# Attention and hidden layer on eight cores: the last two token tiles one by one, bias rows by an accumulating DMA, query weights loaded sooner

## The reference, cut to what matters

```
x = x + attn(layernorm(x))
    q = r @ query_proj (16 heads);  k = r @ key_proj;  v = r @ value_proj
    out = softmax(q k^T / 8) v, then @ output_proj
x = x + ffn(layernorm(x))
    s = r @ Win + bin                      # 64 features
    h = relu(s[..., None] * W1 + b1)       # 64 x 16
    g = sum(h * W2, over the 16) + b2
    out = g @ Wout + bout                  # 1,024 features
```

## Time and profile before

| what | us |
|---|---|
| three runs shown | 969.11, 969.49, 1022.97 (median 969.49) |
| the profiled execution | 971.45 |
| its spans, cores 0 to 7 | 968.6, 967.3, 969.1, 965.8, 969.9, 965.9, 966.7, 966.5 |
| slowest core | core 4, mean granted TensorE clock 0.981 |
| busy on core 4 | PE 900.7, ACT 913.9, DVE 646.1, POOL 72.2 |

### The profile page before, as it was taken

How to read it: one execution, slowest core, us unless ns; L and a number is a source line. 1 busy time by engine, 2 the same in 40 slices (tenths; PEclk the granted TensorE clock), 3 DMA queues, 4 the chain that set the end, 5 groups by cost and what they waited for, 6 DMA issues and landing times.

```text
span 969.9 us, 29153 instructions; the slowest of 8 cores (965.8 to 969.9 us)
## 1 busy us (share of the span) xinstructions
PE 900.7 (93%) x11484; PEld 479.2 (49%) x11484; DVE 646.1 (67%) x938; ACT 913.9 (94%) x1000; POOL 72.2 (7%) x150
## 2 busy tenths in 40 slices
PE   3899999999999999998999999998999998998895
PEld 3445555554445554554555554554454454454442
DVE  4756777522469999988889899658332378748225
ACT  2599999999999999999999999999999999999971
POOL 3211112100000000000010000000000000100000
PEclk9999999999999999999999999999999999999995
DMA  8722346400100010001031000001130100500101
GB/s 194 183 73 89 110 142 135 97 2 2 28 18 19 18 19 17 3 7 51 29 115 18 18 18 14 7 7 50 36 108 18 29 13 7 180 18 18 50 2 44
DMA packets 46291, 48.71 MB, mean 50 GB/s; under 512 B 35152, under 2 KB 35280, under 8 KB 46160
## 3 DMA queue, kind: packets, MB, share of 16 engines
q1 hardware_dynamic: 38352, 27.71, 10.4%
q0 software_dynamic: 7520, 18.62, 7.6%
q10 hardware_dynamic: 288, 0.52, 0.1%
HBM read 35.70 MB, written 8.39 MB: 45 GB/s over the span
## 4 chain that ended last, share of the span: by engine, by line
ACT 78%; issue 11%; PE 7%; DVE 2%; DMA 2%; POOL 0%; DVEq 0%; SPq 0%; ACTq 0%; POOLq 0%
ACT ptu L1163 77%; PE ob L731 2%; DMA xbuf<-x_own 1%; PE spa L1030 1%; DMA wqb<-wq 1%; PE spb L1030 1%; PE spb L1067 0%; PE spa L1067 0%; PE sdb L664 0%; DVE lnst L753 0%; DVE lnst L757 0%; PE sdb L695 0%; PE sda L695 0%; ACT hz L1173 0%; DVE gacc L1132 0%
## 5 line engine op out<-in xcount | busy, mean ns | idle before, releaser
L1163 ACT ACTIVATE ptu<-spa 128x1024 bf16<-128x1024 f32 x491 | 555.3, 1131 | 11.5 <-PE spa L1030 11.3
L1163 ACT ACTIVATE ptu<-spb 128x1024 bf16<-128x1024 f32 x490 | 555.8, 1134 | 3.6 <-PE spb L1030 3.3
L731 PE MATMUL ob<-vab,ptu 128*128 128x65 bf16 x7848 | 391.7, 195 | 3.4 <-DVE oacc L943 1.1
L731 PEld LDWEIGHTS ob<-vab,ptu 128*128 128x128 bf16 x7848 | 286.7, 98 | 203.8 <-issue 203.8
L1030 PE MATMUL spb<-qt,k2t 64*128 64x512 bf16 x980 | 193.5, 382 | 19.4 <-ACT ptu L1163 18.0
L1030 PE MATMUL spa<-qt,k2t 64*128 64x512 bf16 x982 | 193.6, 383 | 17.9 <-ACT ptu L1163 14.9
L1030 PEld LDWEIGHTS spb<-qt,k2t 64*128 64x128 bf16 x980 | 58.7, 92 | 110.7 <-issue 95.9
L1030 PEld LDWEIGHTS spa<-qt,k2t 64*128 64x128 bf16 x982 | 57.7, 93 | 108.5 <-issue 95.0
L943 DVE TENSOR_TENSOR oacc<-oacc,ob 128x520 f32<-128x520 f32 x52 | 35.8, 689 | 76.4 <-PE ob L731 76.3
L1184 POOL TENSOR_SCALAR lnve<-lnmv 128x1 f32<-128x1 f32 x48 | 14.9, 311 | 582.1 <-DVE lnmv L759 582.0
L929 DVE SCALAR_TENSOR_TENSOR r1t<-oacc 128x1024 bf16<-128x1024 f32 x43 | 52.6, 1223 | 5.2 <-DVE oacc L924 4.7
(11 more groups left out here) (136 smaller groups left out, 705.3 us busy)
## 6 DMA issues: line engine op xcount, KB each, us to landing
xbuf<-x_own SPq DMA_DIRECT2D x16, 512.0 KB, 5.2
xbuf<-x_oth SPq DMA_DIRECT2D x16, 512.0 KB, 3.4
out<-xbuf POOLq DMA_DIRECT2D x14, 512.0 KB, 3.1
xbuf<-x_own POOLq DMA_DIRECT2D x12, 512.0 KB, 7.1
wqb<-wq POOLq DMA_DIRECT2D x8, 256.0 KB, 9.3
xtra<-x_own SPq DMA_DIRECT2D x4, 512.0 KB, 6.6
xtra<-wp POOLq DMA_DIRECT2D x8, 256.0 KB, 4.7
ot<-on SPq DMA_TRANSPOSE x38, 2.3
```

The lines of the kernel that those rows point to most:

```text
L731: r = te.matmul(osum[:, hd, c * 65:(c + 1) * 65], ptu[:, g % NPT, hd * 512 + c * 128:hd * 512 + (c + 1) * 128], vab[:, CHUNKS[s][i], :], s ...
L1163: sc.activation(ptu[:, g % NPT, :], sps[g % 2][:], AF.Exp, scale=0.125 / SCORE_SCALE).then_inc(ex, 1)
```

## The change

Five things are changed.

1. GpSimd issues the value weights and query chunk 1 after the root of the second tile, chunk 2 after the third and chunk 3 after the fourth. VectorE normalizes the second tile ahead of the third tile's statistics. `AT_FIRST` is 1.4 us less.
2. The second pass of the final additions is gone. GpSimd issues, once a tile is normalized, a DMA that adds boutbc to the tile in xbuf (both in on-chip memory), and the first final addition of a tile waits for it. The new semaphores stand for four buffers.
3. In the tail the one-row bias matmuls are gone, and tiles 14 and 15 get their bias by the same DMA.
4. In the tail VectorE adds and takes statistics for both tiles, then normalizes both. The hidden layer is computed for one tile after the other, with 128 columns.
5. The four sums of tile 14 stand ahead of VectorE's move of tile 15's transposes, the other twelve behind it.

```diff
-AT_FIRST = {"pe": 2100, "dve": 2200}
+AT_FIRST = {"pe": 1960, "dve": 2060}
...
                     xh = xbuf[:, t, b * 512:(b + 1) * 512]
+                    if b == 0:
+                        v.wait_ge(bad[t], 16 * (a // 4 + 1))
                     v.tensor_tensor(xh, xh, bank[:], op=ALU.add).then_inc(sev, 1)
-                    note("sev", n + 1)
-                    yield [], 75
-                    v.wait_ge(sev, n + 1)
-                    if a == 0 and b == 0:
-                        v.wait_ge(boutl, 16)
-                    v.tensor_tensor(xh, xh, boutbc[:, b * 512:(b + 1) * 512], op=ALU.add).then_inc(bad, 1)
...
-            for n, t in enumerate(GROUPS[-1]):
-                te.wait_ge(xad, n + 1)
-                for h in range(2):
-                    te.matmul(sps[t % 2][:, h * 512:(h + 1) * 512], ones1[:],
-                              boutbc[0:1, h * 512:(h + 1) * 512], start=True, stop=False)
...
+            def hidden(n, t):
+                te.wait_ge([rta, rtv][n], 1)
+                for j in range(DCH):
+                    r = te.matmul(obk[:, 512 * n:512 * n + 128], winb[:, j, :],
+                                  r2t[:, j, t % 4 * 128:t % 4 * 128 + 128],
+                                  start=(j == 0), stop=(j == DCH - 1))
+                r.then_inc(s2t, 1)
...
+            ta, tb = GROUPS[-1]
+            transposes(0, ta)
+            hidden(0, ta)
+            transposes(1, tb)
+            hidden(1, tb)
+            ffn_out(0, ta)
+            ffn_out(1, tb)
...
             ln_stats(v, 1)
             ln_norm(v, 0)
+            ln_norm(v, 1)
             ln_stats(v, 2)
-            ln_norm(v, 1)
             ln_stats(v, 3)
...
                 v.wait_ge(xad, n + 1)
                 ln_stats(v, li)
-                ln_norm(v, li)
+            for t in GROUPS[-1]:
+                ln_norm(v, NTILES + t)
...
+            for p in range(4):
+                hidden_sum(0, p)
             v.wait_ge(rtt, 2)
             v.tensor_copy(r2t[:, :, 384:512], side[1][:, :].bitcast(BF16).rearrange("p (j t) -> p j t", t=128)
                           ).then_inc(rtv, 1)
+            for p in range(4, 8):
+                hidden_sum(0, p)
             for p in range(8):
...
+                hidden_sum(1, p)
+            for n, t in enumerate(GROUPS[-1]):
+                v.wait_ge(bad[t % 4], 16 * NK)
...
+        def add_bout(e, t):
+
+            if t == 0:
+                e.wait_ge(boutl, 16)
+            e.wait_ge(nrm, NTILES + t + 1)
+            e.dma_start(xbuf[:, t % 4, :], boutbc[:], accum_op=ALU.add).then_inc(bad[t % 4], 16)
...
-                if i == 2:
+                if i == 1:
                     e.dma_start(wvb[:], wv_d.rearrange("p (j m) -> p j m", m=64)).then_inc(wvl, 16)
-                for c in {2: [1], 3: [2, 3], 4: [4], 5: [5], 6: [6], 7: [7]}.get(i, []):
+                for c in {1: [1], 2: [2], 3: [3], 4: [4], 5: [5], 6: [6], 7: [7]}.get(i, []):
...
                 for t in ts:
-                    e.wait_ge(bad, 2 * t + 2)
+                    add_bout(e, t)
+                for t in ts:
+                    wait_ev(e, USE_NO["fo", t, 1])
                     e.dma_start(out_r[t], xbuf[:, t % 4, :]).then_inc(ost[t % 4], 16)
```

More of the change, by code:

```diff
@@ L533, in build_nc @@
         rsd = sem("rstd_set")
-        bad = sem("bout_added")
+        bad = [sem(f"bout_added{q}") for q in range(4)]
         b1s = sem("b1adj_set")
@@ L1063, in _, with transposes @@
                 r.then_inc(opt, 1)
-            for n, t in enumerate(GROUPS[-1]):
-                te.wait_ge(xad, n + 1)
-                for h in range(2):
-                    te.matmul(sps[t % 2][:, h * 512:(h + 1) * 512], ones1[:],
-                              boutbc[0:1, h * 512:(h + 1) * 512], start=True, stop=False)
+            def transposes(n, t):
                 te.wait_ge(nrm, NTILES + t + 1)
@@ L1074, in _, with ffn_out @@
                 r.then_inc(rtt, 1)
[L1075 to L1082, removed]
+            def hidden(n, t):
[5 more added lines that the diff above has]
+                r.then_inc(s2t, 1)
+            def ffn_out(n, t):
+                te.wait_ge(g2c, len(GROUPS) + n)
                 for h in range(2):
@@ L1085, in _ @@
                               g2b[:, t % 4 * 128:(t % 4 + 1) * 128], woutb[:, h * 512:(h + 1) * 512],
-                              start=False, stop=True).then_inc(fot, 1)
+                              start=True, stop=True).then_inc(fot, 1)
+            ta, tb = GROUPS[-1]
[5 more added lines that the diff above has]
+            ffn_out(1, tb)
         @block.vector
@@ L1119, in _, with hidden_sum @@
                 ln_stats(v, li)
-                ln_norm(v, li)
+            for t in GROUPS[-1]:
+                ln_norm(v, NTILES + t)
+            def hidden_sum(n, p):
+                cols = slice(128 * n, 128 * n + 128)
+                last = slice(256 + 128 * n, 384 + 128 * n)
+                v.wait_ge(rel, 8 * n + p + 1)
+                dst = g2b[:, last] if p == 7 else gacc[p % 2][:, cols]
+                if p == 0:
+                    v.tensor_scalar(dst, zt[p % 4][:, cols], w2p[:, p:p + 1], b2h[:], op0=ALU.mult,
+                                    op1=ALU.add).then_inc(gtl, 1)
+                else:
+                    v.wait_ge(gtl, 7 * n + p)
+                    v.scalar_tensor_tensor(dst, zt[p % 4][:, cols], w2p[:, p:p + 1],
+                                           gacc[(p + 1) % 2][:, cols],
+                                           op0=ALU.mult, op1=ALU.add).then_inc(g2c if p == 7 else gtl, 1)
+            for p in range(4):
+                hidden_sum(0, p)
             v.wait_ge(rtt, 2)
@@ L1123, in _ @@
                           ).then_inc(rtv, 1)
+            for p in range(4, 8):
+                hidden_sum(0, p)
             for p in range(8):
[L1125 to L1134 removed]
+                hidden_sum(1, p)
+            for n, t in enumerate(GROUPS[-1]):
+                v.wait_ge(bad[t % 4], 16 * NK)
                 for h in range(2):
[L1136 removed]
+                    v.wait_ge(fot, 2 * n + h + 1)
                     xh = xbuf[:, t % 4, h * 512:(h + 1) * 512]
@@ L1168, in _ @@
                           AF.Copy).then_inc(rta, 1)
-            sc.wait_ge(s2t, 1)
-            for p in range(8):
-                if p >= 4:
-                    sc.wait_ge(gtl, p - 3)
-                sc.activation(zt[p % 4], obk[:, 0:256], AF.Relu, bias=b1adj[:, p:p + 1],
-                              scale=w1p[:, p:p + 1]).then_inc(rel, 1)
+            for n in range(2):
+                sc.wait_ge(s2t, n + 1)
+                for p in range(8):
+                    if p >= 4:
+                        sc.wait_ge(gtl, 7 * n + p - 3)
+                    sc.activation(zt[p % 4][:, 128 * n:128 * n + 128], obk[:, 512 * n:512 * n + 128], AF.Relu,
+                                  bias=b1adj[:, p:p + 1], scale=w1p[:, p:p + 1]).then_inc(rel, 1)
             for n, t in enumerate(GROUPS[-1]):
@@ L1221, in _ @@
                 rstd_of(e, NTILES + t)
+            for t in GROUPS[-1]:
+                add_bout(e, t)
             for q in range(4):
+                e.wait_ge(bad[q], 16 * NK)
                 e.wait_ge(ost[q], 16 * (NK if q < 2 else NK - 1))
```

10 lines of the change are left out of this document (removed).

## The result

The changed kernel takes 985.03 us (median of four runs, 984.0 to 987.25), the kernel before 969.55 on the same chip: ratio 1.0159 with an interval of 1.0144 to 1.0174, so 15 us slower. 966.8 was predicted, and a range of 964.0 to 970.2. The direction and the range were wrong; that the time stays within 2%, which had 0.97, was right. (In some executions, such as the 1022.97 shown before, some of the cores ran at a lower clock; these count in the medians that are given, but are left out of all ratios.)

A forecast was written before the change was run, and what follows sets the result against it. ScalarE's exponentials were taken as the bound, leaving only head and tail to shorten. From the median 969.49 us, -1.3 for the head and -1.4 for the tail gave 966.8 us, range 964.0 to 970.2.

The forecast's parts named there:

- Bias rows in the middle: Tiles 0 to 13: accumulating transfers on GpSimd's queue hidden by 35 us of cover before VectorE's final additions; cost 0.
- 28 additions taken off VectorE: Middle: removing 19.4 us of VectorE additions, all beside ScalarE's full stretch, is worth 0.
- Planner's order in the head: Head: the planner's earlier start only reorders VectorE's instructions; cost 0, with 0.7 us either way kept for the range.
- Query weights sooner: Head: second query chunk issued 3.8 us sooner; -2.55 us on core 4, taken as -1.3 on the median.
- rival 1: Head gains nothing because VectorE's order sets it: 968.1 us, or 969.1; chance 0.22 together with another rival.
- The first exponential: Head, sign against the forecast: it is wrong if the first exponential moves to 24 us.
- the 17th: Head of core 4, sign for the forecast: the seventeenth exponential starts between 46 and 47 us.
- Tail: Tiles 14 and 15 handled one by one, sums at a pitch of 0.45 us: last addition ends 1.4 us sooner.
- Rival 2: Tail: accumulating transfer takes twice as long, 14.2 us, delaying the last addition: 969.0 us; chance 0.10.
- Rival 3: Tail: transfer ends the kernel, delaying VectorE's last additions from a 12.0 us landing on; 971.8 at 17 us; chance 0.09.
- A stall in the middle from the new order: Middle: a stall caused by the new order of work; chance 0.03.
- The forecast's own span: Whole kernel: 964.8 to 968.1 us, from head 0 to -2.55 and tail pitch 0.38 to 0.50.

The follow-up runs named there:

- kernel 5: kernel 2 with GpSimd's four loads of tiles 12 to 15 issued behind the landing of the head-output transposes needed for tile 12: 970.07 us, ratio 1.0001.
- kernel 2: The changed kernel with a group's accumulating transfers issued only after VectorE has moved that group's hidden layer input (s2): 974.88 us, ratio 1.0038.
- kernel 1: The changed kernel without the 14 accumulating transfers of tiles 0 to 13, their bias rows left out: 975.98 us, ratio 1.0051.
- kernel 7: The kernel before with the whole new head, AT_FIRST included, and the new tail; middle bias additions stay on VectorE: 969.94 us, ratio 1.0002.
- kernel 6: The kernel before with the new tail, sooner weight loads and second normalization, but old AT_FIRST and middle bias additions on VectorE: 967.89 us, ratio 0.9979.
- kernel 9: kernel 5 with the old AT_FIRST, so all three costly places of the changed kernel are mended: 967.93 us, ratio 0.9973.
- kernel 4: The kernel before with the new tail alone; old head, bias additions of the other tiles on VectorE: 969.22 us, ratio 0.9982.
- Kernel 3: The kernel before with only the 28 middle bias additions moved from VectorE to accumulating transfers, old head and tail: 985.76 us, ratio 1.0151.

## Why the prediction was wrong

**Bias rows in the middle: this step failed.** It said "35 us of cover" and "Four of 7.1 us one after the other (28.4) are hidden: 0". The size was near (8.4 us against 7.1, though an issue took GpSimd 0.99 us and not 0.6) and VectorE's final additions never waited. But the cover was counted for the transfer's own reader. The 16 DMA engines also carried a transposition issued 1.6 us behind, which TensorE needed 8 us later. That wait, the third group's twin at 893 us and the lower clock behind both cost 11.7 us (1.0159 to 1.0038 when the same transfers are issued later; 10.5 when they are left out).

**28 additions taken off VectorE: "worth 0", and it was a loss.** It was right that ScalarE cannot gain from it. What the step left out is what a sooner end of VectorE's work starts: the loads of tiles 12 to 15, 1.8 in place of 5.4 us behind the transposes. 3.6 us by kernel 5 against 2, 4.8 us by kernel 1 against 7 (1.0051 to 1.0002).

**Planner's order in the head, "I cost the order at 0"**, 0.7 us either way: wrong, it costs 2.2 us (kernels 6 and 7; 2.7 by kernels 5 and 9), in one gap more and two longer ones. The cover named, that VectorE has work meanwhile, says nothing of who waits for the piece that now comes later.

**Query weights sooner, -1.3 on the median:** the weights were in time on every core, as said. The gain measured is 0.3 us (kernels 4 and 6), with an uncertainty of some 1.4 us when both intervals are taken together, so neither the 1.3 nor the 0 of rival 1 is excluded. In kernel 4, with the old head, core 2 has its 17th exponential at 46.09 us, against 48.96 in the profile of before: how long a core waits for weights differs from one execution to the next, and one slow core of one profile was no measure of the median. The first exponential, named as a sign at 24 us, came at 22.6 to 24.6 us over the changed kernel's cores and at 22.7 to 24.2 in kernel 4, with the old head, so it is no sign of the new one. In the changed kernel the 17th came at 47.5 to 49.5 us and not at 46 to 47. It came 24.9 us after the first on every core; before it was 23.4 to 24.2 us on the five cores that did not wait for weights and 25.9 to 26.2 on the three that did.

**Tail, -1.4:** right in mechanism and in size, -1.7 [-2.7, -0.8] on the chip, 22.67 - 20.81 = 1.9 us in the traces. The pitch taken, 0.45, was 0.454. The bias rows were needed some 11 us after their issue and landed in 5.3 and 5.8. The first ReLU came 4.0 us sooner behind the addition of tile 14, and 3.8 was forecast (behind the last exponential).

**Rivals.** Rival 2's mechanism holds: an accumulating transfer alone takes 5.5 us, a plain copy 3.1, 1.8 times as long. The Trainium skill, "Collectives: The Full Stack", on why reduce-scatter is slower than all-gather, says about half the rate; the 1.8 here comes near it. It did no harm in the tail, where it was expected. Rival 3 did not come; GpSimd's issue beside a normalization took 1.21 us and the other 0.86. "A stall in the middle from the new order" had 0.03, and the second hole is such a stall; the larger part of the loss is the collision of transfers, which no case named.

**Sum by the runs:** +11.7 for the transfers, +3.6 for the loads, +2.2 for AT_FIRST, -1.7 for the tail and -0.3 for the weights make +15.5; measured +15.4. Each term has an uncertainty of 1 to 2 us, and some compare kernels on different chips, so that close a match is in part luck. Kernel 3 is a check from outside: the transfers and the loads make 15.3, and the middle alone measured +14.6 (13.0 to 16.2).

**A bound of the range.** The forecast's own span, 964.8 to 968.1, takes the head and the pitch one at a time; both at their ends give 969.49 - 2.55 - 1.4 - 1.1 = 964.4 and 969.49 - 1.4 + 0.8 = 968.9. Both lie inside the stated range, so nothing hung on it.

## What to carry to other kernels

A new transfer is hidden only if every other transfer in flight with it is hidden too: list what else is issued within its landing time, on any queue, and who waits for that, small transposes first. Work that is taken off an idle engine moves whatever its end releases. When a collision can't be avoided, put the large transfer behind the wait that the small one feeds, as kernels 2 and 5 do.

## What the runs showed of the hardware

- A DMA transposition of 128 x 1,024 bf16 (1,056 packets) lands in 3.0 or 3.1 us alone. With two accumulating transfers of 512 KB in flight it took 7.2 to 8.6 us, with four 8.0 to 8.3 in the first two groups and 13.5 to 14.0 in the third, and with four plain copies in the third 11.2 to 13.0.
- An accumulating transfer of 512 KB within on-chip memory lands in 5.5 us alone and in 8.5 in the median of four; a plain copy in 3.1 and 5.8. Issuing four takes GpSimd 3.97 us, four plain ones 2.76.
- TensorE's waits of 5.6 to 6.2 us were followed on all eight cores by matmuls of 0.58 to 0.62 us in place of 0.38 (the lower level of the clock), on core 2 for 3.5 us, with gaps of 0.50 us ahead of the exponentials; there the stretch from 800 to 808 us was granted 0.79. Of waits near 2 us some were and some were not: behind 1.96 us on core 2 the scores took 0.61 us, behind 2.17 us on core 6 the stretch from 840 to 856 us was granted 1.00.
